# Attention passes of 512 queries instead of 1024, with four similarity tiles and two accumulators in turn

## What is computed

```
q, k, v = (LN(xn) @ Wq, @ Wk, @ Wv)          # [2048, 16, 64] each
q, k    = q/|q|, k/|k|
state   = q
for _ in range(2):                            # two steps
    sim   = state . k        (per head, 2048 x 2048)
    state = softmax(sim) . v
s = xn + state @ Wo
```

## Time and profile before

| | us |
|---|---|
| median of 2 runs | 12663.22 (12624.07 and 12702.37) |
| the profiled execution | 12684.37 |
| its span, slowest core (7) | 12682.8 |
| spans of the 8 cores | 12460.5 to 12682.8 |
| mean granted clock of TensorE, by core | 0.733 to 0.761 of full speed |

### The profile page before, as it was taken

The page is one execution under the profiler, slowest core; times in us unless marked ns, Lnnn a source line. Parts: engine busy times, 40 slices in busy tenths (PEclk is TensorE's granted clock), DMA queues, the critical chain, the costliest instruction groups (busy, mean ns, idle before and its releaser), DMA issues.

```text
span 12682.8 us, 90463 instructions; the slowest of 8 cores (12460.5 to 12682.8 us)
## 1 busy us (share of the span) xinstructions
PE 8468.4 (67%) x28800; PEld 2974.0 (23%) x28800; DVE 3294.2 (26%) x5341; ACT 3265.3 (26%) x3764; POOL 70.6 (1%) x137
## 2 busy tenths in 40 slices
PE   3666776666568883888536667776666688838785
PEld 2222222111123331333222222211111233313331
DVE  5221111111133332333352211111111233323333
ACT  1114555555200000000011145555552000000000
POOL 0000000000000000000000000000000000000000
PEclk6667777777767885888756567777777678858897
DMA  3100000000211101111121000000001111111111
GB/s 86 23 8 0 0 0 0 0 0 0 65 25 23 28 17 58 23 23 28 42 87 23 8 0 0 0 0 0 0 0 57 33 23 25 21 58 23 24 28 46
DMA packets 77408, 287.73 MB, mean 23 GB/s; under 512 B 8826, under 2 KB 17172, under 8 KB 66708
## 3 DMA queue, kind: packets, MB, share of 16 engines
q0 software_dynamic: 19040, 130.84, 5.4%
q1 hardware_dynamic: 57908, 151.10, 3.6%
HBM read 354.03 MB, written 58.72 MB: 33 GB/s over the span
## 4 chain that ended last, share of the span: by engine, by line
PE 54%; ACT 17%; DVE 16%; issue 7%; DMA 4%; SPq 1%; DVEq 1%; ACTq 1%; POOLq 0%
ACT arena L625 12%; PE psa L848 8%; PE psb L848 8%; PE psa L901 6%; PE psa L631 4%; PE psb L901 4%; PE psa L582 4%; PE psb L609 4%; DMA arena<-x 2%; PE psa L484 2%; PE psb L883 1%; DVE arena L872 1%; DVE arena L891 1%; DVE arena L587 1%; DVE arena L916 1%
## 5 line engine op out<-in xcount | busy, mean ns | idle before, releaser
L625 ACT ACTIVATE arena<-psb 128x1024 bf16<-128x1024 f32 x2048 | 2097.7, 1024 | 1407.0 <-PE psb L609 1198.2
L609 PE MATMUL psb<-arena 65*128 65x512 bf16 x4096 | 1498.5, 460 | 291.1 <-ACT arena L648 251.8
L631 PE MATMUL psa<-arena 128*65 128x512 bf16 x4096 | 1431.2, 436 | 351.9 <-ACT arena L625 157.3
L848 PE MATMUL psa<-arena 128*128 128x512 bf16 x4096 | 1053.4, 404 | 125.6 <-DVE arena L916 111.0
L848 PE MATMUL psb<-arena 128*128 128x512 bf16 x4096 | 1055.2, 405 | 0.0
L867 ACT ACTIVATE arena<-psa 128x512 f32<-128x512 f32 x256 | 152.9, 597 | 3221.9 <-PE psa L855 3209.8
L642 DVE COPY arena<-psa 65x1024 f32<-65x1024 f32 x128 | 156.3, 1221 | 2941.8 <-PE psa L631 2941.8
L901 PE MATMUL psa<-arena 128*128 128x512 bf16 x2048 | 740.1, 541 | 120.9 <-DVE arena L891 120.9
L582 PE MATMUL psa<-arena,onescf 1*64 1x512 f32 x512 | 490.9, 1059 | 467.7 <-DVE arena L590 153.9
L609 PEld LDWEIGHTS psb<-arena 65*128 65x128 bf16 x4096 | 451.0, 113 | 1030.9 <-issue 737.8
L631 PEld LDWEIGHTS psa<-arena 128*65 128x65 bf16 x4096 | 362.6, 120 | 1400.0 <-issue 1369.0
(11 more groups left out here) (162 smaller groups left out, 6357.6 us busy)
## 6 DMA issues: line engine op xcount, KB each, us to landing
arena<-wfs POOLq DMA_DIRECT2D x64, 1728.0 KB, 11.5
arena<-x SPq DMA_DIRECT2D x96, 512.0 KB, 3.9
xnsp<-arena SPq DMA_DIRECT2D x64, 256.0 KB, 3.0
arena<-xnsp SPq DMA_DIRECT2D x16, 1024.0 KB, 6.9
ssp<-arena SPq DMA_DIRECT2D x64, 256.0 KB, 2.9
arena<-ssp SPq DMA_DIRECT2D x32, 512.0 KB, 4.1
out<-arena SPq DMA_DIRECT2D x32, 512.0 KB, 2.9
nxsp<-arena SPq DMA_DIRECT2D x64, 128.0 KB, 3.3
```

What stands on the lines that cost most here:

```text
L609: T(lambda e, c=c, sb=sb, j2=j2, qco=qco, stin=stin, kaug=kaug: e.matmul(psb[:, 1024 * sb + 512 * j2:1024 * sb + 512 * (j2 + 1)], kaug[0:6 ...
L625: SC(lambda e, ab=ab, sb=sb: e.activation(att[ab], psb[:, 1024 * sb:1024 * sb + HL], AF.Exp), waits=[(tc_, simv[c])] + att_rel[ab], inc=sc)
L631: T(lambda e, c=c, ab=ab, j2=j2, hh=hh: e.matmul(psa[0:65, 512 * j2:512 * (j2 + 1)], vbuf[:, 1040 * c + 65 * hh:1040 * c + 65 * (hh + 1)], ...
L848: wslb=wslb, tco=tco: e.matmul(grp(bank_i), wslb[:, FC * c + 128 * m:FC * c + 128 * (m + 1)], nxh[:, TH * c + tco:TH * c + tco + TC], star ...
```

## The change

`HL` becomes 512, so a head has `NQH` = 4 passes of 512 queries. The similarity tiles are 128 x 512 and there are four of them, one in each bank of `psb`; four are issued ahead instead of two. Each exponential is 128 x 512. The accumulators of successive passes lie in banks 0 and 1 of `psa` in turn (`sp = qh % 2`), and the first accumulating matmul of a pass waits for the copy that last emptied its own bank (`st_rel[sp]`). Each accumulating matmul now raises TensorE's counter. The copy L642, the two ScalarE instructions behind it, and the product in `flush_tail` are over 512 columns and there are twice as many. `flush_tail` itself isn't edited: by its loops over `NQH` and `HL // 512` it issues four times (matmul, copy, product) where it issued twice (matmul, copy, matmul, copy, product). The waits of the first similarity matmuls of a pass are still set to `sc.v`.

```diff
-    HL = min(S, 1024)
+    HL = min(S, 512)
...
+        st_rel = [[(vc, 0)], [(vc, 0)]]
...
-                    sim_rel = [[(sc, sc.v)], [(sc, sc.v)]]
+                    sp = qh % 2
+                    sim_rel = [[(sc, sc.v)] for _ in range(4)]
                     att_rel = [[(tc_, tc_.v)] for _ in range(4)]
-                    acc_gate = [(vc, vc.v)]
+                    acc_gate = st_rel[sp]
 
                     def emit_sim(c):
-                        sb = c % 2
-                        for j2 in range(HL // 512):
-                            T(lambda e, c=c, sb=sb, j2=j2, qco=qco, stin=stin, kaug=kaug: e.matmul(
-                                psb[:, 1024 * sb + 512 * j2:1024 * sb + 512 * (j2 + 1)],
...
+                        sb = c % 4
+                        T(lambda e, c=c, sb=sb, qco=qco, stin=stin, kaug=kaug: e.matmul(
+                            psb[:, 512 * sb:512 * (sb + 1)],
+                            kaug[0:65, 128 * c:128 * (c + 1)],
+                            stin[0:65, qco:qco + HL],
+                            start=True, stop=True),
+                          waits=[head_in] + sim_rel[sb], inc=tc_)
                         return tc_.v
 
                     simv = [0] * n_tt
-                    simv[0] = emit_sim(0)
-                    if n_tt > 1:
-                        simv[1] = emit_sim(1)
+                    for cpre in range(min(4, n_tt)):
+                        simv[cpre] = emit_sim(cpre)
                     for c in range(n_tt):
-                        sb = c % 2
-                        ab = c % 4
-                        SC(lambda e, ab=ab, sb=sb: e.activation(att[ab], psb[:, 1024 * sb:1024 * sb + HL],
-                                                                AF.Exp),
-                           waits=[(tc_, simv[c])] + att_rel[ab], inc=sc)
+                        sb = c % 4
+                        SC(lambda e, sb=sb: e.activation(
+                            att[sb], psb[:, 512 * sb:512 * (sb + 1)], AF.Exp),
+                           waits=[(tc_, simv[c])] + att_rel[sb], inc=sc)
...
+                        T(lambda e, c=c, sb=sb, sp=sp, hh=hh: e.matmul(
+                            psa[0:65, 512 * sp:512 * sp + HL],
+                            vbuf[:, 1040 * c + 65 * hh:1040 * c + 65 * (hh + 1)],
+                            att[sb],
+                            start=(c == 0), stop=(c == n_tt - 1)),
+                          waits=[(sc, scv)] + (acc_gate if c == 0 else []),
+                          inc=tc_)
+                        att_rel[sb] = [(tc_, tc_.v)]
+                        if c + 4 < n_tt:
+                            simv[c + 4] = emit_sim(c + 4)
                     st_ready = tc_.v
-                    V(lambda e, z=z, qco=qco: e.tensor_copy(
-                        stg[z][:, qco:qco + HL], psa[0:65, 0:HL]),
-                      waits=[(tc_, st_ready)])
+                    V(lambda e, z=z, qco=qco, sp=sp: e.tensor_copy(
+                        stg[z][:, qco:qco + HL], psa[0:65, 512 * sp:512 * sp + HL]),
+                      waits=[(tc_, st_ready), (tc_, tc_.v)])
+                    st_rel[sp] = [(vc, vc.v)]
```

More of the change, by code:

```diff
@@ L628, in build_program @@
                         scv = sc.v
                         sim_rel[sb] = [(sc, scv)]
[L630 to L637, removed]
@@ L638, in build_program @@
-                        att_rel[ab] = [(tc_, tc_.v)]
-                        if c + 2 < n_tt:
-                            simv[c + 2] = emit_sim(c + 2)
+                        T(lambda e, c=c, sb=sb, sp=sp, hh=hh: e.matmul(
[5 more added lines that the diff above has]
+                          inc=tc_)
```

## The result

| | before | after |
|---|---|---|
| median of the runs, us | 12662.7 (10 runs) | 13363.4 (11 runs) |
| ratio after / before | | 1.047, 95% interval 1.038 to 1.056 |
| profiled execution, us | 12684.4 | 13169.95 |
| span of core 0 in it, us | 12486.2 | 13143.4 |
| exponentials, count x mean ns | 2048 x 1024 | 4096 x 597 |

The change makes the kernel about 5% slower.

What follows compares the result with a forecast made beforehand. It took TensorE to bind a pass at low clock, ScalarE at high clock, then a chained pause. Longer heads add 32 × 20.8 = + 666 us to 12684; less 21 over the median, 13,330 us; range 13,150 to 13,480.

Steps and rivals of the forecast that it cites:

- ScalarE's step: In attention, each 512-column exponential plus the gap behind it takes 0.745 us, thus 1.49 us for 1024 columns.
- ScalarE alone sets the pass, at either clock: Within an attention pass, four tiles' head start hides TensorE's slow part, so ScalarE's 0.745 us steps set the pace.
- The pause: Between passes of a head, the chain to the next exponential stays but shrinks from 5.67 to 3.64 us.
- The end of a head: The gap behind a head's last pass, with flush_tail, becomes 16.38 us in step 0 and 26.96 in step 1.
- Heads: An attention head takes 74.4 us in step 0 against 63.44, and 85.0 in step 1 against 75.08.
- The time: The whole kernel takes 13,330 us, 5% slower, from + 666 us in attention.
- TensorE binds: Rival, 10%: in attention passes the high clock isn't granted and TensorE sets the pace, + 143 us, 13,470 us.
- The other side: Rival, 3%: ScalarE's start-up overlaps, exposing only 0.43 us a step in attention passes, − 900 us, 12,430 us.
- The passes overlap after all: Rival, 3%: all three pauses inside a head vanish, 700 us less, 12,630 us, no change.
- the 8.3 us of low clock: Start of an attention pass before the change: TensorE at about 1.2 GHz for 8.27 us, with 5 exponentials.

Runs made afterwards that it cites:

- e7: The changed kernel, with exponentials that don't wait for the ScalarE instruction before them; ratio 1.019 to the kernel before, attention 522 us less than after.
- e3: The changed kernel with sim_rel and att_rel carried from pass to pass; ratio 1.043 to the kernel before, attention 130 us less than after.
- e4: e3 with Ln and Exp of row 64 done once a head instead of once a pass; ratio 1.023 to the kernel before.
- e9: e4 with the next pass's similarity matmuls issued block by block in the pass before; ratio 1.010 to the kernel before.
- e6b: The changed kernel with exponentials over only 256 of each tile's 512 columns; ratio 1.019 to the kernel before, attention 530 us less than after.
- e5b: The kernel before (1024-query passes) with the same three edits as e9 and two accumulators of 1024 columns; ratio 0.968 to the kernel before.
- e12: e5b with exponentials that don't wait for the ScalarE instruction before them; ratio 0.962 to the kernel before.
- e11: e9 with exponentials that don't wait for the ScalarE instruction before them; median 11840 us against 12558 of the kernel before.

## Why the prediction was right, point by point

- **ScalarE's step**: 0.745 us predicted, (11.76 − 0.60) / 15 = 0.744 measured, from the duration of another line's 128x512 instruction and the gap of the earlier trace rows.
- **ScalarE alone sets the pass, at either clock**: right, the merged row of 16 exponentials shows no stop, and the mean body of a pass on core 0 is 11.82 us against the 11.77 predicted. Two small things weren't foreseen. In some passes the clock falls again near the end, and the last matmul takes longer (0.61 instead of 0.38 us above). And 60 of the exponentials inside the passes start some 0.43 us behind the one before instead of 0.147, with their inputs ready; together that is 17 us. They are the same 60 on cores 0 and 5 and lie multiples of some 128 rows of ScalarE's stream apart (128, 255, 384, ...), whatever the place in the pass. Their cause stays open.
- **The pause**: 3.64 us predicted. The one shown is 3.87, behind that late matmul; over the 192 inner pauses of core 5 the median is 3.63 and the mean 3.70. Copies of neighbouring passes: 15.39 us between those at 1712.32 and 1727.71 against 15.41 predicted, 15.51 in the mean, from 15.2 to 15.9.
- **The end of a head**: 11.77 + 16.38 = 28.15 us predicted for step 0, about 28.5 measured between the copies.
- **Heads**: 74.4 and 85.0 us predicted, 75.1 and 85.5 measured. The sum was + 666 us, attention took + 702.
- **The time**: 13,330 us said, 13363 measured. That these lie only 33 us apart is luck in part, as the executions of after range from 13170 to 13546 us; in ratios 1.053 was said and 1.047 measured. The sturdier comparison is 666 with 702.
- **TensorE binds** (rival): no, ScalarE never waits for it inside the pass shown. The worry that the high level would not be granted at 57% load was wrong: on core 0 it was granted in each of the 256 passes, 7.5 us behind the first exponential at the latest, before the tile k = 12 at which the prediction had TensorE fall behind.
- **The other side** (rival): its overlap exists but for the own wait, as e7 shows. My arithmetic for it, − 900 us, needed the clock to hold over the pause. In after it holds in none of them: the granted clock is at the low level at the first exponential of each pass of core 0. e7 gave − 522.
- **The passes overlap after all** (rival): no; e3, e4 and e9 show that three things hold them apart one behind the other: the carried value `sc.v`, Ln and Exp in ScalarE's stream, and the last accumulating matmul in TensorE's.

One number of the prediction was wrong and didn't show in its sum: the 8.3 us of low clock, read from a single pass. With it a head would be 2 × 21.0 + 5.67 + 16.52 = 64.2 us, and it is 63.44. By the clock's own records in the trace that pass has 7.95 us from its first exponential to the rise of the clock, while the mean of the 128 passes on that core is 6.7, from 4.7 to 10.0 (6.5 in first passes of a head, 6.9 in second ones). The very next pass shows how it varies: its first matmul starts at 1733.00, and by 1739.46 a pair takes 0.60 us.

```profile
1738.77 0.85 PE L631 MATMUL psa<-arena 128*65 128x512 bf16 x2
...
1739.46 0.60 PE L609 MATMUL psb<-arena 65*128 65x512 bf16 x2
```

The sum was safe from this as it was made against whole heads. The expectations for e6b, e7 and e5b were built on the 8.3 us. For e6b and e7 that is about half of what was missing, for e5b all of it.

## What to carry to other kernels

Price an instruction by its step, with the wait behind it, not by its duration: halving a tile left 58% of the duration here, but 63% of the step (0.744 of 1.172 us), and doubled the number of short chains between passes. If a stage is an alternation of two bounds, an engine at one clock and another engine at the other, find which one each edit touches; narrow exponentials cost + 454 us and short passes + 692, and both together + 702. More buffers help only once nothing else orders the stream: the form with four narrow tiles was the slower one until the pauses and the own wait were gone, and then it was the faster of the two (1800 against 1973 us of attention). Read a stretch that varies, such as the low clock behind a pause, from many passes before building on it: three of the expectations above rested on one.

## What the hardware showed that I had not expected

- TensorE's clock fell inside a pass in which it is never idle for more than 0.4 us: matmuls of 0.38 us, then 0.49 and 0.61 at the end of a pass that followed a pause of some 3.8 us. The clock fell again before the last exponential ended in 36 of the 256 passes of core 0. With no pauses (e9), at the same pace of one block in 0.744 us, it stayed at 1.00 for the 40 us read.
- In e12 two exponentials of 1.02 us together take 1.94 us, and in e11 23 of 0.60 us take 11.47: behind one another without a wait between them, ScalarE's instructions overlap by 0.1 us, at both widths.
